# Response phase of a fused attention and ConvNeXt block: high half as a view of the product, low half on VectorE, two-bank gelu and output

## The chip, the core and the metric

The kernel runs on one NeuronCore of a Trainium2 chip. The metric is the device time of the whole program in microseconds (us). Three runs of the kernel before took 2929.64, 2929.57 and 2919.75 us, median 2929.57. One more execution was taken by the profiler; every duration below comes from it.

Names of engines: PE is TensorE (PEld its weight loads), DVE is VectorE, ACT is ScalarE, POOL is GpSimd, SP is SyncE, which only issues DMAs here.

## What is computed

The input has 8 images of 48 channels and 112 x 112 pixels. The first layer is a shifted-window attention block with a 48-192-48 MLP. The second is a ConvNeXt V2 block, and the change touches only its end:

```
y = dwconv7x7(x) + dw_b                       # NCHW, then channels last
y = (y - mean) * rsqrt(var + 1e-6) * ln_g + ln_b
y = gelu(y @ w1.T + b1)                       # 48 -> 192 features
gx = sqrt(sum over the image of y*y)          # one number per feature and image
nx = gx / (mean over features of gx + 1e-6)
y = grn_g * (y * nx) + grn_b + y
out = x + (y @ w2.T + b2)                     # 192 -> 48
```

The second matmul of an image can't begin before the squares of all its pixels are added up, because nx depends on the whole image.

## The kernel before

The program has three phases, one after the other: attention, convolution, response. The response phase (`response_phase`) does what stands above from the normalisation on. An image is cut into 8 strips (STRIPS) and there are N = 64 strips. A strip holds 7 rows of the upper half of the image and 7 of the lower half; the halves are groups g = 0 and 1, at partitions 0 to 48 and 64 to 112, and each has 784 pixels (STRIP), cut into two times 392 (HALF), since a PSUM bank holds 512 float32 values.

Every engine walks over the same steps s = -2 ... N+LAG-1 with an order written out by hand in its `step` function, and the engines meet at counting semaphores. LAG is 10: in step s a strip s gets its first matmul (fc1), and strip s-10 ("old") gets its second (fc2), by when its image is summed. G, the gelu's output, has a ring of 16 strips. So there are three stretches: a fill (steps 0 to 9, fc1 alone), a main part (steps 10 to 63, both) and a drain (steps 64 to 73, fc2 alone). In every eighth step `respond` turns the summed squares of an image into scaled second weights; I call this an image boundary.

In one step:

- SP loads Y (the convolution's output) and RS (its 1/std) for strip s+2, and X2, the block's input, for the old strip.
- DVE multiplies Y by RS into `xh` (float32) and casts it to `xm[0]` (bfloat16, the high half) (`normalise`). POOL subtracts, `xm[1] = xh - xm[0]` (`low`), which is the low half. fc1 is then three bfloat16 matmuls, high by high, low by high, high by low, in float32 accuracy.
- PE does fc1 in three parts t = 0, 1, 2, each with two banks b. Parts 0 and 1 make the first 128 features of the two groups for half t of the pixels (in `ps_f[t]`); their two banks use different row groups of the array, and run side by side. Part 2 makes the last 64 features of both groups (in `ps_m`). The step's order on PE is fc1 part 0, fc2 of the old strip, fc1 part 1, fc1 part 2. fc2 is in float32, reads G, and adds up in the two banks of `ps_o`, of which there is one buffer.
- ACT puts the gelu of each bank into G, six instructions of 392 columns (`features`), and squares and sums group 0's 128 first features (`sum_squares`, 784 columns).
- DVE squares and sums the other two thirds of G (group 1's 128 features, and the last 64 of both groups), one 784-column instruction each, and makes the output from `ps_o`, one instruction for each bank (`finish`).
- POOL issues the two stores of the output.

Of the kernel before, what the change touches and what calls it, by code (L numbers as in the profile page):

```python
# [21 lines left out]
STRIP = WS * IMG  # L22
# [1274 lines left out]
def response_phase(nc, weights, later, x2_dram, y_dram, rs_dram, out_dram, strips):  # L1297

    with ExitStack() as ctx:
        def sb(name, shape, dt=F32):  # L1300
            return ctx.enter_context(nc.sbuf_tensor(name, shape, dt))
# [26 lines left out]
        junk_act = sb("r_junk_act", [128, STRIP])  # L1328
        sums = sb("r_sums", [128, 3, RING])
        total = sb("r_total", [128, 3])  # L1330
        both = sb("r_both", [128, 2])
# [8 lines left out]
        S = sems("cleared y_cleared setup_v setup_t f1 f2 pairs mean_ps xh hi summed summed_act totals "  # L1340
# [25 lines left out]
        def _(sp):  # L1366
# [3 lines left out]
            def step(s):  # L1370
# [10 lines left out]
                if old.real:  # L1381
                    if isinstance(old.n, int) and old.n == 0:
                        wait(sp, S["cleared"], CLEARS)
                    wait(sp, S["out_made"], 2 * (old.n - 1))
# [8 lines left out]
        def _(pool):  # L1393
# [3 lines left out]
            def low(s):  # L1397
                if s.real:
                    wait(pool, S["hi"], s.n + 1)
                    wait(pool, S["f1"], 6 * (s.n - 1))  # L1400
                    nc.gpsimd.tensor_tensor(xm[1][:, s.slot(2), :], xh[:], xm[0][:, s.slot(2), :],  # L1401
                                            ALU.subtract).then_inc(S["lo"], 1)

            def store(s):
                if s.real:
                    wait(pool, S["out_made"], 2 * s.n + 2)
# [13 lines left out]
        def _(dve):  # L1420
# [43 lines left out]
            def sum_squares(s, t):  # L1464

                if s.real:
                    wait(dve, S["ge"], 6 * s.n + (4 if t < 2 else 6))
                    g = G[:, s.raw % RING, t, :]
                    wait(dve, S["summed"], 2 * s.n + t - 1)
                    nc.vector.tensor_tensor_reduce(out=junk[:], in0=g, in1=g, scale=1.0, scalar=0.0, op0=ALU.mult,  # L1470
                                                   op1=ALU.add, accum_out=sums[:, t, s.raw % RING:s.raw % RING + 1]
# [305 lines left out]
```

## Time and profile before

| what | value |
|---|---|
| runs | 2929.64, 2929.57, 2919.75 us, median 2929.57 |
| profiled execution | 2942.04 us, its span 2940.4 us |
| granted PE clock, mean over the span | 0.931 |
| busy over the span | PE 2583.5 (88%), DVE 2032.3 (69%), ACT 1767.5 (60%), POOL 1337.5 (45%) |
| response phase, first fc1 to last output instruction | 2485.4 to about 2926 us after the start |

The page divides the whole program. The response phase is its last 15%, so a busy share of the span says little on it, and the rows below are cut to stretches of the phase. Time runs from the start of the span. A clock of 1.00 is 2.4 GHz, and 0.50 is 1.2 GHz.

### The profile page before, as it was taken

The numbers are of one execution on the slowest core, as the hardware profiler recorded it, in microseconds if no ns is written. First come the engines' busy times: TensorE is split into PE (matmuls) and PEld (weight loads), VectorE is DVE, ScalarE is ACT, GpSimd is POOL, SyncE is SP. The second block draws the span as 40 slices with busy tenths as digits, with TensorE's granted clock in tenths as the row PEclk, the third lists the DMA queues.
The fourth block names the chain that finished last, engine by engine and source line by source line (L and its number), as shares of the span: only waits on it lengthen the run. The fifth ranks groups of instructions, "written<-read, shape, count | busy, mean of one in ns | idle before, by whom it ended". The sixth has DMA issues, their size and how long they took to land. (4 is left out here: it accounts for less than half of the span.)

```text
span 2940.4 us, 81102 instructions
## 1 busy us (share of the span) xinstructions
PE 2583.5 (88%) x30330; PEld 1517.3 (52%) x30330; DVE 2032.3 (69%) x3231; ACT 1767.5 (60%) x3278; POOL 1337.5 (45%) x1333
## 2 busy tenths in 40 slices
PE   3999899898989898998989899899937996889997
PEld 2666565565656565565656556566513553333332
DVE  3767676666666675676667667667568996988984
ACT  1666565565656565565656566566657775655551
POOL 3555454454445454454545445455311333544552
PEclk9989999999899999999999999999958998889988
DMA  3111111111111111111111111111036995777774
GB/s 41 31 27 27 35 32 27 27 33 33 27 27 27 34 33 27 27 39 27 27 27 39 27 27 33 34 27 34 20 70 190 287 288 140 158 179 181 193 173 119
DMA packets 198492, 209.90 MB, mean 71 GB/s; under 512 B 159246, under 2 KB 160131, under 8 KB 198184
## 3 DMA queue, kind: packets, MB, share of 16 engines
q1 hardware_dynamic: 185896, 166.14, 24.1%
q0 software_dynamic: 12288, 39.07, 4.3%
q8 instruction: 264, 4.33, 0.6%
q14 instruction: 44, 0.36, 0.0%
HBM read 124.64 MB, written 80.58 MB: 70 GB/s over the span
## 5 line engine op out<-in xcount | busy, mean ns | idle before, releaser
L348 POOL TENSOR_TENSOR shift<-const_b,qmax 113x588 bf16<-113x588 bf16 x256 | 314.2, 1227 | 253.3 <-DVE qmax L536 253.3
L337 POOL TENSOR_TENSOR xm_l<-xh,xm_h 113x784 bf16<-113x784 f32 x128 | 214.6, 1676 | 463.5 <-DVE xm_h L456 463.5
L647 ACT ACTIVATE P<-ps_t 98x588 f32<-98x588 f32 x256 | 169.6, 662 | 337.9 <-PE ps_t L839 337.3
L375 POOL TENSOR_TENSOR sqb_l<-sq,sqb_h 113x392 bf16<-113x392 f32 x256 | 259.7, 1034 | 142.7 <-DVE sqb_h L439 142.7
L446 DVE TENSOR_TENSOR xh<-xc,rs 113x784 f32<-113x784 f32 x64 | 62.4, 976 | 349.1 <-ACT rs L632 349.0
L678 ACT ACTIVATE G<-ps_m 128x392 f32<-128x392 f32 x384 | 176.4, 501 | 130.9 <-PE ps_m L896 93.8
L830 PE MATMUL ps_t<-u_h,xs_h 113*98 113x147 bf16 x1024 | 222.9, 233 | 0.0
L830 PE MATMUL ps_t<-u_h,xs_l 113*98 113x147 bf16 x1024 | 222.5, 232 | 0.0
L830 PE MATMUL ps_t<-u_l,xs_h 113*98 113x147 bf16 x1024 | 222.4, 232 | 0.0
L536 DVE TENSOR_REDUCE qmax<-ps_s 113x12 f32<-113x588 f32 x256 | 196.3, 767 | 36.4 <-PE ps_s L809 33.4
L639 ACT CAST u_h<-ps_m 113x392 bf16<-113x392 f32 x384 | 177.4, 479 | 67.6 <-PE ps_m L784 66.1
L825 PE MATMUL ps_t<-bias,const_b 113*98 113x294 bf16 x512 | 155.4, 303 | 70.5 <-issue 69.4
L629 ACT ACTIVATE lnv<-ps_m,eps 113x392 f32<-113x392 f32 x256 | 138.6, 584 | 130.2 <-PE ps_m L731 128.6
L385 POOL TENSOR_TENSOR x1b_l<-x,x1b_h 113x392 bf16<-113x392 f32 x128 | 119.0, 930 | 213.0 <-DVE x1b_h L563 213.0
L1556 ACT ACTIVATE r_G<-r_ps_f 128x392 f32<-128x392 f32 x256 | 113.9, 511 | 158.2 <-PE r_ps_f L1607 157.9
L528 DVE TENSOR_TENSOR u_l<-ps_m,u_h 113x392 bf16<-113x392 f32 x384 | 199.2, 556 | 7.6 <-ACT u_h L639 7.6
L1238 PE MATMUL conv_ps<-xp_h,band_now 128*64 128x448 bf16 (+1 forms) x1536 | 189.7, 355 | 16.8 <-DVE band_now L1136 16.8
L1470 DVE CUSTOM_DVE_ANT_0 r_junk<-r_G 128x784 f32<-128x784 f32 x128 | 194.1, 1516 | 5.1
L839 PE MATMUL ps_t<-shift,const_b 113*98 113x294 bf16 x512 | 115.1, 308 | 77.5 <-POOL shift L348 76.6
L1096 POOL DMA_DIRECT2D y_scratch<-y x144 | 75.3, 523 | 219.6 <-ACT y L1183 211.2
L809 PE MATMUL ps_s<-xm_h,u_h 49*49 49x49 bf16 x6144 | 174.8, 186 | 0.0
L1408 POOL DMA_DIRECT2D out_rolled<-r_OUT x128 | 80.5, 633 | 206.7 <-DVE r_OUT L1518 206.4
(252 smaller groups left out, 7941.7 us busy)
## 6 DMA issues: line engine op xcount, KB each, us to landing
xin<-rows_scratch SPq DMA_DIRECT2D x96, 236.0 KB, 5.0
xin<-rows_scratch SPq DMA_DIRECT2D x96, 235.8 KB, 5.3
X<-x_windows SPq DMA_DIRECT2D x128, 147.0 KB, 2.9
x_scratch<-x SPq DMA_DIRECT2D x128, 147.0 KB, 2.8
y_scratch<-y POOLq DMA_DIRECT2D x96, 196.0 KB, 4.2
r_RS<-rs_scratch SPq DMA_DIRECT2D x128, 147.0 KB, 3.5
r_Y<-y_scratch SPq DMA_DIRECT2D x128, 147.0 KB, 3.8
r_X<-x_scratch SPq DMA_DIRECT2D x128, 147.0 KB, 4.0
```

The costliest lines, as they stand in the source:

```text
L337: nc.gpsimd.tensor_tensor(xm[a][1][:, r, :], xh[a][:], xm[a][0][:, r, :], ALU.subtract).then_inc(S["lo"][a], 1)
L348: nc.gpsimd.tensor_tensor(shift[:, j % 2], e, m, ALU.mult).then_inc(S["md"], 1)
L375: nc.gpsimd.tensor_tensor(sqb[a][1][:, cols], sq[a][:, cols], sqb[a][0][:, cols], ALU.subtract).then_inc(S["sq_lo"][a], 1)
L528: nc.vector.tensor_tensor(U[1][:, r, h, cols], ps_m[0:R, b, 0:HALF], U[0][:, r, h, cols], ALU.subtract).then_inc(S["u_lo"], 1)
L536: nc.vector.tensor_reduce(qmax[:, j % 2, :].rearrange("p (b n) -> p b n", b=2), ps_s[0:R, :, 0:2 * HQ].rearrange("p b (n t) -> p b n t", t ...
L639: nc.scalar.copy(U[0][:, s.slot(2), h, HALF * b:HALF * b + HALF], ps_m[0:R, b, 0:HALF]).then_inc(S["u_hi"], 1)
L647: nc.scalar.activation(P[:, j % 2].rearrange("p (b n) h t -> p b (n h t)", b=2), ps_t[0:KEYS, :, 0:2 * HQ], ACT.Exp).then_inc(S["ex"], 1)
L678: nc.scalar.activation(out, ps_m[:, b, 0:HALF], ACT.Gelu).then_inc(S["ge"], 1)
L809: ins = mm(ps_s[lo:lo + TOK, b, at:at + TOK], U[0][lo:lo + C + 1, r, h, TOK * w:TOK * w + TOK], xm[0][0][lo:lo + C + 1, r, TOK * w:TOK * w ...
L830: mm(ps_t[0:KEYS, b, HQ * k:HQ * k + HQ], xs[ws][:, r, w, :], U[ms][:, r, :, TOK * w:TOK * w + TOK], start=False, stop=False)
L1238: ins = mm(ps[s][SIDE * side:SIDE * side + SIDE, k, 0:half * IMG], band_now[0:rows_, s, w, m, :], xp[part][0:rows_, s, side, half * k:half ...
L1470: nc.vector.tensor_tensor_reduce(out=junk[:], in0=g, in1=g, scale=1.0, scalar=0.0, op0=ALU.mult, op1=ALU.add, accum_out=sums[:, t, s.raw % ...
```

## The change

Five things change, all in the response phase. (1) `xh` becomes a double buffer in float32, and the high half is no tile of its own any more: `x_high` is a view of `xh` that takes the upper two bytes of each float32 value, so it is cut off and not rounded. fc1's moving operand then has a step of 4 bytes. (2) The low half is subtracted on DVE, not on POOL. POOL only issues stores in the loop. (3) ACT squares both groups' first 128 features in one instruction of 1568 columns, and DVE only squares the last 64. (4) The gelu takes both banks of a part in one instruction, so ACT waits for both, and fc1 for both to be read. (5) The output of a strip is one DVE instruction over both banks, so it waits for both halves of fc2, and fc2 of the next strip waits for all of it. The sums have two columns, and the small addition after the reduction goes.

```
-        xh = sb("r_xh", [R, STRIP])
-        xm = [sb(f"r_xm_{p}", [R, 2, STRIP], BF16) for p in "hl"]
+        xh = sb("r_xh", [R, 2, STRIP])
+        x_low = sb("r_x_low", [R, 2, STRIP], BF16)
+        x_high = xh[:].bitcast(BF16).rearrange("p r (n t) -> p r n t", t=2)[:, :, :, 1]
+        xm = (x_high, x_low)
...
-            def low(s):
-                if s.real:
-                    wait(pool, S["hi"], s.n + 1)
-                    wait(pool, S["f1"], 6 * (s.n - 1))
-                    nc.gpsimd.tensor_tensor(xm[1][:, s.slot(2), :], xh[:], xm[0][:, s.slot(2), :],
-                                            ALU.subtract).then_inc(S["lo"], 1)
...
                     wait(dve, y_loaded[r], 64 * (s.turn(2) + 1))
-                    wait(dve, S["lo"], s.n)
-                    nc.vector.tensor_tensor(xh[:], Y[:, r, :], RS[:, r, :], ALU.mult).then_inc(S["xh"], 1)
+                    wait(dve, S["f1"], 6 * (s.n - 1))
+                    nc.vector.tensor_tensor(xh[:, r, :], Y[:, r, :], RS[:, r, :], ALU.mult).then_inc(S["xh"], 1)
                     wait(dve, S["xh"], s.n + 1)
-                    wait(dve, S["f1"], 6 * (s.n - 1))
-                    nc.vector.tensor_copy(xm[0][:, r, :], xh[:]).then_inc(S["hi"], 1)
+                    nc.vector.tensor_tensor(x_low[:, r, :], xh[:, r, :], x_high[:, r, :], ALU.subtract).then_inc(S["lo"], 1)
...
-                    for b in range(2):
-                        cols = slice(HALF * b, HALF * b + HALF)
-                        wait(dve, S["f2"], 2 * s.n + b + 1)
-                        nc.vector.scalar_tensor_tensor(
-                            out=OUT[:, s.slot(2), cols], in0=ps_o[0:n, b, 0:HALF], scalar=out_b[:, 0:1],
-                            in1=X2[:, s.slot(2), cols], op0=ALU.add, op1=ALU.add).then_inc(S["out_made"], 1)
+                    wait(dve, S["f2"], 2 * s.n + 2)
+                    nc.vector.scalar_tensor_tensor(
+                        out=halves(OUT[:, s.slot(2), :]), in0=ps_o[0:n, :, 0:HALF], scalar=out_b[:, 0:1],
+                        in1=halves(X2[:, s.slot(2), :]), op0=ALU.add, op1=ALU.add).then_inc(S["out_made"], 1)
...
-                    nc.scalar.activation(junk_act[:], G[:, slot, 0, :], ACT.Square,
+                    nc.scalar.activation(junk_act[:], G[:, slot, 0:2, :], ACT.Square,
...
-                    for b in range(2):
-                        wait(act, S["f1"], 6 * s.n + 2 * t + b + 1)
-                        cols = slice(HALF * (t if t < 2 else b), HALF * (t if t < 2 else b) + HALF)
-                        nc.scalar.activation(G[:, slot, b if t < 2 else 2, cols],
-                                             ps_f[t][:, b, 0:HALF], ACT.Gelu).then_inc(S["ge"], 1)
+                    wait(act, S["f1"], 6 * s.n + 2 * t + 2)
+                    out = G[:, slot, 0:2, HALF * t:HALF * t + HALF] if t < 2 else halves(G[:, slot, 2, :])
+                    nc.scalar.activation(out, ps_f[t][:, :, 0:HALF], ACT.Gelu).then_inc(S["ge"], 1)
...
-                    for b in range(2):
-                        wait(pe, S["out_made"], 2 * (s.n - 1) + b + 1)
+                    wait(pe, S["out_made"], s.n)
+                    for b in range(2):
                         cols = slice(HALF * b, HALF * b + HALF)
```

On DVE the main part's step read as follows before (r_OUT is the output, the rows ISA are the squares and the reading of their sum):

```order
L1518 SCALAR_TENSOR_TENSOR r_OUT<-r_ps_o,r_out_b,r_X 112x392 [waits r_f2,r_stored0,r_x2_loaded0]
L1518 SCALAR_TENSOR_TENSOR r_OUT<-r_ps_o,r_out_b,r_X 112x392 [waits r_f2]
L1459 TENSOR_TENSOR r_xh<-r_Y,r_RS 113x784 [waits r_lo,r_y_loaded0]
L1462 CAST r_xm_h<-r_xh 113x784 [waits r_f1,r_xh]
L1470 ISA r_junk,r_sums<-r_G 128x784 [waits r_summed,r_ge]
L1470 ISA r_sums 128x1
L1470 ISA r_junk,r_sums<-r_G 128x784 [waits r_summed,r_ge]
L1470 ISA r_sums 128x1
```

and the same step of the kernel after on DVE (the L46 rows only set a register or wait):

```order
L1505 SCALAR_TENSOR_TENSOR r_OUT<-r_ps_o,r_out_b,r_X 112x784 [waits r_f2]
L46 ISA
L46 REGISTER_ALU [waits r_y_loaded0]
L1452 TENSOR_TENSOR r_xh<-r_Y,r_RS 113x784 [waits r_f1]
L46 REGISTER_ALU
L1454 TENSOR_TENSOR r_x_low<-r_xh 113x784 [waits r_xh]
L46 ISA
L1462 ISA r_junk,r_sums<-r_G 128x784 [waits r_summed,r_ge]
L1462 ISA r_sums 128x1
```

One output instruction and one square are gone, the cast has become a subtraction, and the wait for fc1 (r_f1) now stands ahead of the product.

On PE the end of the drain read, before (r_w2s are the scaled second weights):

```order
L1640 MATMUL r_ps_o<-r_G,r_w2s_both 112x392 [waits r_out_made]
L1643 MATMUL r_ps_o<-r_G,r_w2s_own 48x392 x2
L1640 MATMUL r_ps_o<-r_G,r_w2s_both 112x392 [waits r_out_made]
L1643 MATMUL r_ps_o<-r_G,r_w2s_own 48x392 x2
L1299 UNCONDITIONAL_BRANCH
```

and after:

```order
L1623 MATMUL r_ps_o<-r_G,r_w2s_both 112x392 [waits r_out_made]
L1626 MATMUL r_ps_o<-r_G,r_w2s_own 48x392 x2
L1623 MATMUL r_ps_o<-r_G,r_w2s_both 112x392
L1626 MATMUL r_ps_o<-r_G,r_w2s_own 48x392 x2
L1299 UNCONDITIONAL_BRANCH
```

The number of matmuls is the same; the wait for the output now stands once for a strip, ahead of its first bank, and the strip before must be read out whole by then.

## Rows read from the trace of the kernel before

**Rows 1.** By stretch: length, busy us (instructions), clock, DMA share, GB/s.

```profile
core 0: us, PE busy (x) PEld busy (x) DVE busy (x) ACT busy (x) POOL busy (x), PEclk, DMA share, GB/s
2485.00:2535.00 50.00, 35.69 (x194) 15.53 (x194) 44.17 (x63) 38.20 (x86) 24.63 (x12) 0.70 0.72 143
...
2530.00:2880.00 350.00, 321.20 (x1638) 109.10 (x1640) 308.73 (x479) 191.11 (x442) 173.83 (x157) 0.92 0.74 180
...
2600.00:2634.00 34.00, 34.00 (x184) 11.25 (x183) 33.03 (x46) 20.03 (x50) 18.84 (x18) 1.00 0.82 202
...
2903.00:2928.00 25.00, 22.28 (x83) 5.92 (x82) 8.76 (x14) 0.00 (x0) 7.96 (x16) 1.00 0.54 163
```

**Rows 2.** Timeline, PE in one step: start, us, instruction, [idle before it].

```profile
2604.74 0.35 PE L1607 MATMUL r_ps_f<-r_xm_h,r_w_own_h 49*128 49x392 bf16 x2
...
2607.06 0.91 PE L1640 MATMUL r_ps_o<-r_G,r_w2s_both 128*112 128x392 f32 x2
...
2610.34 0.35 PE L1607 MATMUL r_ps_f<-r_xm_h,r_w_own_h 49*128 49x392 bf16 x2
```

**Rows 3.** Timeline, DVE and POOL in the same step.

```profile
2605.01 1.15 DVE L1518 SCALAR_TENSOR_TENSOR r_OUT<-r_ps_o,r_out_b,r_X 112x392 f32<-112x392 f32 x2
...
2606.08 0.96 DVE L1459 TENSOR_TENSOR r_xh<-r_Y,r_RS 113x784 f32<-113x784 f32 x1
...
2607.17 0.57 DVE L1462 CAST r_xm_h<-r_xh 113x784 bf16<-113x784 f32 x1
...
2607.65 0.97 DVE L1470 CUSTOM_DVE_ANT_0 r_junk<-r_G 128x784 f32<-128x784 f32 x1
...
2608.36 1.79 POOL L1401 TENSOR_TENSOR r_xm_l<-r_xh,r_xm_h 113x784 bf16<-113x784 f32 x1
...
2608.67 2.32 DVE L1470 CUSTOM_DVE_ANT_0 r_junk<-r_G 128x784 f32<-128x784 f32 x1
...
2610.92 1.15 DVE L1518 SCALAR_TENSOR_TENSOR r_OUT<-r_ps_o,r_out_b,r_X 112x392 f32<-112x392 f32 x2
```

**Rows 4.** Timeline, ACT in the same step.

```profile
2605.44 0.89 ACT L1556 ACTIVATE r_G<-r_ps_f 128x392 f32<-128x392 f32 x2 [2.33 <-PE r_ps_f L1607]
...
2606.97 0.88 ACT L1543 ACTIVATE r_junk_act<-r_G 128x784 f32<-128x784 f32 x1
...
2607.72 0.22 ACT L1543 ACTIVATION_READ_ACCUMULATOR r_junk_act<-r_G 128x1 f32 x1
```

**Rows 5.** Timelines of PE and DVE at the image boundary near 2583 us.

```profile
2582.66 0.38 PE L1622 MATMUL r_ps_o<-r_total,r_eye 128*128 128x1 f32 x2 [1.41 <-DVE r_OUT L1518]
```

```profile
2585.30 0.16 DVE L1494 TENSOR_SCALAR r_mean<-r_ps_o 128x1 f32<-128x1 f32 x1 [0.22 <-PE r_ps_o L1628]
...
2585.69 0.93 DVE L1499 SCALAR_TENSOR_TENSOR r_scale<-r_gx,r_inv,r_grn_g 128x2 f32<-128x2 f32 x1
```

```profile
2587.43 1.64 PE L1640 MATMUL r_ps_o<-r_G,r_w2s_both 128*112 128x392 f32 x2 [2.17 <-DVE r_w2s_both L1507]
...
2590.48 1.65 PE L1640 MATMUL r_ps_o<-r_G,r_w2s_both 128*112 128x392 f32 x2
```

**Rows 6.** Timeline of the drain.

```profile
2896.04 0.16 DVE L1494 TENSOR_SCALAR r_mean<-r_ps_o 128x1 f32<-128x1 f32 x1 [1.63 <-PE r_ps_o L1628]
...
2896.43 0.22 DVE L1499 SCALAR_TENSOR_TENSOR r_scale<-r_gx,r_inv,r_grn_g 128x2 f32<-128x2 f32 x1
...
2897.38 1.65 PE L1640 MATMUL r_ps_o<-r_G,r_w2s_both 128*112 128x392 f32 x2 [1.37 <-DVE r_w2s_both L1507]
...
2903.85 0.91 PE L1640 MATMUL r_ps_o<-r_G,r_w2s_both 128*112 128x392 f32 x2
...
2907.12 0.91 PE L1640 MATMUL r_ps_o<-r_G,r_w2s_both 128*112 128x392 f32 x2
2907.34 0.62 DVE L1518 SCALAR_TENSOR_TENSOR r_OUT<-r_ps_o,r_out_b,r_X 112x392 f32<-112x392 f32 x1 [1.11 <-PE r_ps_o L1643]
```

**Rows 7.** A moving operand with 4-byte steps (the convolution's fill): timeline and stretch.

```profile
2180.89 0.53 PE L1223 MATMUL conv_ps<-split,hot 71*64 71x192 bf16 x4 [1.26 <-DVE band L1128]
```

```profile
2180.00:2190.00 10.00, 2.65 (x20) 0.92 (x20) 10.00 (x7) 10.00 (x7) 0.00 (x0) 0.50 0.09 20
```

More of the change, by code:

```diff
@@ L1323, in response_phase @@
         RS = sb("r_RS", [R, 2, STRIP])
-        xh = sb("r_xh", [R, STRIP])
-        xm = [sb(f"r_xm_{p}", [R, 2, STRIP], BF16) for p in "hl"]
+        xh = sb("r_xh", [R, 2, STRIP])
+        x_low = sb("r_x_low", [R, 2, STRIP], BF16)
+        x_high = xh[:].bitcast(BF16).rearrange("p r (n t) -> p r n t", t=2)[:, :, :, 1]
+        xm = (x_high, x_low)
         G = sb("r_G", [128, RING, 3, STRIP])
         junk = sb("r_junk", [128, STRIP])
[L1328 to L1331, printed above, removed]
+        junk_act = sb("r_junk_act", [128, 2, STRIP])
+        sums = sb("r_sums", [128, 2, RING])
+        total = sb("r_total", [128, 2])
         gx = sb("r_gx", [128, 2])
@@ L1383, in step @@
                         wait(sp, S["cleared"], CLEARS)
-                    wait(sp, S["out_made"], 2 * (old.n - 1))
+                    wait(sp, S["out_made"], old.n - 1)
                     for g in range(2):
@@ L1457, in normalise, with sum_squares @@
                     wait(dve, y_loaded[r], 64 * (s.turn(2) + 1))
[L1458 to L1459 removed]
+                    wait(dve, S["f1"], 6 * (s.n - 1))
+                    nc.vector.tensor_tensor(xh[:, r, :], Y[:, r, :], RS[:, r, :], ALU.mult).then_inc(S["xh"], 1)
                     wait(dve, S["xh"], s.n + 1)
[L1461 to L1464 removed]
+                    nc.vector.tensor_tensor(x_low[:, r, :], xh[:, r, :], x_high[:, r, :], ALU.subtract).then_inc(S["lo"], 1)
+            def sum_squares(s):
                 if s.real:
[L1467 to L1469 removed]
+                    wait(dve, S["ge"], 3 * s.n + 3)
+                    g = G[:, s.raw % RING, 2, :]
+                    wait(dve, S["summed"], s.n)
                     nc.vector.tensor_tensor_reduce(out=junk[:], in0=g, in1=g, scale=1.0, scalar=0.0, op0=ALU.mult,
[L1471 removed]
+                                                   op1=ALU.add, accum_out=sums[:, 1, s.raw % RING:s.raw % RING + 1]
                                                    ).then_inc(S["summed"], 1)
@@ L1480, in add_up @@
                     img, p = image(s), s.raw // STRIPS % 2
-                    wait(dve, S["summed"], 2 * (s.n + STRIPS))
+                    wait(dve, S["summed"], s.n + STRIPS)
                     wait(dve, S["summed_act"], s.n + STRIPS)
                     nc.vector.tensor_reduce(total[:], sums[:, :, STRIPS * p:STRIPS * (p + 1)], AX_X, ALU.add
-                                            ).then_inc(S["totals"], 1)
-                    wait(dve, S["totals"], 2 * img + 1)
-                    nc.vector.tensor_tensor(total[:, 0:1], total[:, 0:1], total[:, 1:2], ALU.add
                                             ).then_inc(S["totals"], 1)
@@ L1528, in step @@
                 normalise(nx2)
-                sum_squares(prv, 1)
             steps(dve, step, N + LAG)
@@ L1597, in fc1 @@
                     if t == 0:
-                        wait(pe, S["hi"], s.n + 1)
                         wait(pe, S["lo"], s.n + 1)
@@ L1601, in fc1 @@
                     ps = ps_f[t]
+                    wait(pe, S["ge"], 3 * (s.n - 1) + t + 1)
                     for b in range(2):
-                        wait(pe, S["ge"], 2 * (3 * (s.n - 1) + t) + b + 1)
                         for k, (w, m) in enumerate(((0, 0), (0, 1), (1, 0))):
@@ L1619, in respond @@
                     if part == 0:
-                        wait(pe, S["totals"], 2 * img + 2)
-                        wait(pe, S["out_made"], 2 * s.n)
+                        wait(pe, S["totals"], img + 1)
+                        wait(pe, S["out_made"], s.n)
                         mm(ps_o[:, 0, HALF:HALF + 1], eye[:], total[:, 0:1], start=True, stop=True)
-                        mm(ps_o[:, 0, HALF + 1:HALF + 2], twins[:], total[:, 2:3], start=True, stop=True
+                        mm(ps_o[:, 0, HALF + 1:HALF + 2], twins[:], total[:, 1:2], start=True, stop=True
                            ).then_inc(S["pairs"], 1)
@@ L1636, in fc2 @@
                     slot = s.raw % RING
+                    wait(pe, S["out_made"], s.n)
                     for b in range(2):
-                        wait(pe, S["out_made"], 2 * (s.n - 1) + b + 1)
                         cols = slice(HALF * b, HALF * b + HALF)
```

13 lines of the change are left out of this document (6 added, 7 removed).

## The prediction

> **What bounds the kernel now.** I read the share by slices first, to see where the response phase lies, then the phase by stretches, then the timelines of one ordinary step, one image boundary and the drain. The whole phase is 441 us of a span of 2940.4 us, so even a tenth of it is 1.5% of the time.
>
> In the main part 350 us hold PE 321 busy at a clock of 0.92 and DVE 309, while ACT has 191 and POOL 174 [rows 1]. Between boundaries, as from 2600 to 2634, PE is busy in every microsecond at full clock. So an ordinary step is bound by PE: the first matmul of fc1 part 1 stands at 2604.74 and again at 2610.34, a period of 5.60 us, of which fc2 is 3.28 (2607.06 to 2610.34) and fc1 2.32 [rows 2]. The reader is to see that DVE's own period is longer: 2605.01 to 2610.92, 5.91 us without a gap [rows 3]. DVE loses 0.31 us a step on PE and pays at the next image boundary, where PE has to wait for it.
>
> Why DVE is so full stands in the same rows. A square of 784 columns takes 0.97 us, and the second one 2.32, though it is the same instruction. POOL's subtraction runs from 2608.36 to 2610.15, and the long square from 2608.67 ends 0.84 after it [rows 3]. It waited 1.35 us for POOL.
>
> At a boundary PE waits 1.41 us for the late output before it can add up the sums (2582.66), and again until the scaled weights are there at 2587.43, 4.77 us later. By then its clock is at half: one bank of fc2 takes 3.05 us (2587.43 to 2590.48) against 1.64, half of 3.28 [rows 2, 5].
>
> **The main part, ordinary steps: 0.** DVE's new step, from rows 3: one square 0.97 and its read 0.11; the product 0.96; the subtraction, which no row has on DVE, taken as the product's 0.96 with 0.12 of waiting between them (the cast came 1.09 after the product's start, 0.13 after its end); the output in one piece, between 1.15 (two pieces as now) and 0.62 plus 0.41 for 392 more columns at the slope of the cheap square, so 1.03. Sum 4.2 us, and no POOL operation to collide with. If the subtraction cost as much as the long square, 2.32, it would be 5.5, still below 5.60; if it went like the cast, 3.8. ACT: two gelus of 392 take 0.89 together, one of 784 about the square's 0.88; spaced as the square and its read are (0.75) that is 2.25 for three, the square of 1568 columns 1.4 to 1.5, the read 0.1, together 3.8 of 5.60 [rows 4]. So both engines lie under PE, whose matmuls are the same in number and size. The waits that are now for both banks fall on buffers that are read long before: ACT idles 2.33 us in each step. What DVE gives back in ordinary steps is worth nothing. Between 0 and -0.1 us a step for PE; I take 0.
>
> The wait for fc1 now stands ahead of the product. Behind it are queued the subtraction and the square; the product is for strip s+2, whose fc1 comes more than one whole step of 5.60 us later, and 3 us are enough. SP's loads wait for the product and so start about 1 us later relative to fc2; they have two steps to land.
>
> **Seven boundaries with fc1 beside them: -19 us, and -7 for the clock.** The DVE lag of 7 x 0.31 = 2.2 us is gone, so the output is ready 1.3 us after fc2's end (worked out under the drain), while fc1's parts 1 and 2, nine of its twelve streams, take 1.7 of the 2.32. The first wait goes: -1.4 (Rows 5 has a typical one). From the adding-up (T) on: DVE does the product and the subtraction first, which wait for fc1 and take 0.96 + 0.12 + 0.96, until T+2.2. Then comes the chain from the mean to the weights. In the drain, with no POOL operation beside it, it takes 1.34 us (2896.04 to 2897.38), its L1499 0.22; at the boundary the same L1499 took 0.93 [rows 5, 6]. So fc2 starts at T+3.5, not T+4.77: -1.3. Together -2.7 a boundary, seven times -19. If DVE were still late by a square (0.97), -1.7 each and -12.
>
> The clock: of PE's idle time of 3.6 us at this boundary, about 1.5 is left. At half clock fc2 of that step costs up to 2 x (3.05 - 1.64) = 2.8 us more; since the clock comes back within it in most cases, I take 2 us for each. If the clock no longer falls that is -14, if it falls as before 0. I take half, -7.
>
> **Fill: -5 us.** In the fill a step had no output, so DVE needed 5.91 - 1.15 = 4.76 us, and PE ran at a mean clock of 0.70 [rows 1, 3]. The new bound is ACT's 3.8 us, or PE at half clock with twice 2.32, less its fixed gaps, 4.2; I take 4.0. That is 0.75 for each of the seven steps in which both squares ran. The first three were shorter already. Bounds: 0 (loads can't follow; their share is 0.72 at 4.76 us a step, 0.86 at 4.0) and -9.
>
> **Drain: +11 us, and +2 for the clock.** Here nothing covers the output. Before, PE filled one bank while DVE read the other, and fc2 of a strip took 3.28 us without a gap (2903.85 to 2907.12) [rows 6]. Now fc2 of the next strip waits for the whole output: DVE started 0.22 us after PE had gone on (2907.34 against 2907.12), then come 1.03 for the output and some 0.05 for the way back, an estimate: 1.3 us. Of ten strips eight have such a transition without fc1 or a boundary in it: +10.4, and the last output ends 0.4 later. With 1.15 for the output it is +12; with the 0.62 of one bank, which is too little, +7.
>
> A rule speaks against the change here. The Trainium skill, TensorE: Matmul & The Clock Gate, section A second HAM failure mode: psum-queue depth-cycling, says that short idle times of PE between groups of matmuls that cycle through PSUM banks make its clock swing between its two levels. By that rule the drain would lose more than its gaps. The trace of before is in favour of it in the fill, where the mean clock is 0.70, and can't show it in the drain, where PE has no gaps and a clock of 1.00 [rows 1].
>
> **Sum.** -19 - 7 - 5 + 11 + 2 = -18 us. The profiled execution took 2942.04, its span 2940.4, so it would become 2924. It stands 12.5 us (0.4%) above the median of the runs. On the median, 2929.57 - 18 = 2912 us.
>
> **The rivals.**
>
> A: as summed, 2912, its own range 2900 to 2921. Chance 0.52.
>
> B: the clock stays up at the boundaries. -19 - 14 - 5 + 11 = -27, 2902. For it: only 1.5 of 3.6 us idle are left. Against it: the rest of that stretch is one-column matmuls and weight loads. Chance 0.13.
>
> C: the clock swings in the drain. fc2 of a strip then takes 6.1 instead of 3.28, for up to ten strips +28, with half of them +14, and no gain at the boundaries: -19 - 5 + 11 + 14 = +1, 2930. For it the fill's 0.70, against it that PE is busy for 3.28 of 4.6 us here. Chance 0.13.
>
> D: the loads become the bound. Their share is 0.82 at 5.6 to 5.9 us a step [rows 1] and would be 0.87 at 5.60. X2 of the old strip is issued last and later than now by 1 us; if the output waits for it by over 1 us, PE waits too. With 5.9 us a step, 54 steps x 0.3 = +16 and the sum is -2, 2928. Chance 0.11.
>
> E, the other side: the view with 4-byte steps streams more slowly. Eight of a step's twelve streams of 392 columns read it (parts 0 and 1 two each, part 2 four), each 392 / 2.4 GHz = 0.163 us. At half rate that is +1.3 us a step and +83 in all, 2995. It turns the sum positive from 18 / 64 = 0.28 us a step, 0.035 us a stream. Against it: the convolution's fill has such an operand, four matmuls of 192 columns, two by two side by side, from start to end in 0.53 us at half clock, which is 0.16 for one stream (192 / 1.2 GHz) and a last one's length [rows 7]. So at 1.2 GHz there is no loss; at 2.4 GHz no row shows a bfloat16 view, but fc2's float32 operand also takes 4 bytes a column. Chance 0.06, and 0.05 for any other loss of some size (the subtraction with its strided operand above 2.5 us would make DVE the bound).
>
> **How the numbers follow.** 0.5% of the median is 14.6 us, about what can be told from no change; faster means under 2914.9. Of A's 0.52 some 0.40 lie under it, all of B: 0.53. A's rest, C and D are the same: 0.36. Slower has E and the rest: 0.11. The range for 8 in 10 reaches from B with its bounds, 2893, to C, D and the runs' own scatter of 10 us, 2933.
>
> **What would show it.** In the profile after: DVE's squares all near 0.97 us; a PE step of 5.60 between boundaries with DVE idle in it; no wait of PE's L1605 (the adding-up) for the output; about 3.5 us from there to fc2; in the drain a gap of 1.3 us before each strip's first L1623 and output instructions of about 1.0 us. It is wrong if a stream of x_high takes over 0.17 us at full clock, if DVE waits for X2, or if the drain's clock is 0.50.

## The result, and the profile after

Seven runs of the kernel after took 2895.08 to 2914.46 us, median 2901.78; seven of the kernel before, beside them, 2918.78 to 2940.01, median 2926.01. The ratio is 0.992 with a 95% interval of 0.9891 to 0.995: faster by 0.8%, 24 us (by the interval 15 to 32). The forecast was 2912 us (18 us less) in a range of 2893 to 2933. Ratios leave out runs that took over 1.5% more than the fastest of the same kernel: one of the fourteen of `e1` below, and one of the seventeen of before beside it.

The profiled executions differ by more, a span of 2895.2 against 2940.4 us. But 21 of those 45 us lie ahead of the response phase, where nothing was changed: its first matmul came at 2464.2, before at 2485.4. So I compare the phase by itself. Let R be the time from the first matmul of fc1 to the end of the last output instruction. R fell from 440.6 to 416.6 us, by 24.0. All readings below are of R and its parts, each from one profiled execution:

| kernel | R | fill, to the first fc2 | from an image's first fc2 to the next one's, seven times | last image's first fc2 to the end |
|---|---|---|---|---|
| before | 440.6 | 49.9 | 52.1 53.5 53.4 53.0 51.9 52.8, 45.4 | 28.6 |
| after | 416.6 | 40.8 | 49.8 48.0 49.1 49.6 48.0 48.0, 45.2 | 38.2 |

The windows of the kernel after, in the columns of [rows 1]: fill, main part, an ordinary stretch, drain.

```profile
2470.00:2499.00 29.00, 20.20 (x147) 7.95 (x145) 23.14 (x32) 29.00 (x41) 0.00 (x0) 1.00 0.95 174
2490.00:2840.00 350.00, 330.44 (x1755) 112.26 (x1751) 228.22 (x336) 241.75 (x311) 55.13 (x111) 0.99 0.85 191
2560.00:2594.00 34.00, 34.00 (x184) 11.01 (x182) 23.35 (x31) 23.18 (x31) 6.03 (x13) 1.00 0.91 207
2850.00:2880.00 30.00, 22.20 (x82) 5.75 (x78) 6.43 (x7) 0.00 (x0) 5.97 (x13) 1.00 0.42 129
```

In the main part DVE went from 309 busy us of 350 to 228 and ACT from 191 to 242; PE is at 0.99 of its clock, before at 0.92 [rows 1]. (This window starts 26 us after the first fc1 and that of before 45 us; from 2509 on, at the same distance, it is DVE 220, ACT 225 and a clock of 0.99.) In the drain PE is busy in only 22.2 of 30 us. An ordinary step on PE, which answers to [rows 2]:

```profile
2560.47 0.91 PE L1623 MATMUL r_ps_o<-r_G,r_w2s_both 128*112 128x392 f32 x2
...
2563.75 0.35 PE L1590 MATMUL r_ps_f<-r_xh,r_w_own_h 49*128 49x392 bf16 x2
...
2566.12 0.58 PE L1623 MATMUL r_ps_o<-r_G,r_w2s_both 128*112 128x392 f32 x1
```

The step is 5.65 us (2560.47 to 2566.12) instead of 5.60. fc2 still takes 3.28 of it, so the 0.05 lies in fc1. DVE in the same step, the answer to [rows 3]:

```profile
2559.95 0.97 DVE L1452 TENSOR_TENSOR r_xh<-r_Y,r_RS 113x784 f32<-113x784 f32 x1 [0.71 <-PE r_ps_m L1594]
2560.96 0.97 DVE L1454 TENSOR_TENSOR r_x_low<-r_xh 113x784 bf16<-113x784 f32 x1
2561.86 0.97 DVE L1462 CUSTOM_DVE_ANT_0 r_junk<-r_G 128x784 f32<-128x784 f32 x1
...
2563.86 1.03 DVE L1505 SCALAR_TENSOR_TENSOR r_OUT<-r_ps_o,r_out_b,r_X 112x784 f32<-112x784 f32 x1 [1.03 <-PE r_ps_o L1626]
```

DVE is now idle for 1.74 us of each step; the output takes 1.03 and starts 0.11 after fc2's end at 2563.75. ACT, the answer to [rows 4], does three gelus and the long square, and idles 1.8:

```profile
2560.67 1.50 ACT L1529 ACTIVATE r_junk_act<-r_G 128x1568 f32<-128x1568 f32 x1
...
2562.17 0.81 ACT L1541 ACTIVATE r_G<-r_ps_f 128x784 f32<-128x784 f32 x1
2564.52 0.82 ACT L1541 ACTIVATE r_G<-r_ps_f 128x784 f32<-128x784 f32 x1 [1.54 <-PE r_ps_f L1590]
2565.60 0.82 ACT L1541 ACTIVATE r_G<-r_ps_m 128x784 f32<-128x784 f32 x1 [0.26 <-PE r_ps_m L1594]
```

An image boundary, the answer to [rows 5]:

```profile
2551.37 0.28 PE L1605 MATMUL r_ps_o<-r_total,r_eye 128*128 128x1 f32 x2
...
2552.57 0.97 DVE L1454 TENSOR_TENSOR r_x_low<-r_xh 113x784 bf16<-113x784 f32 x1
...
2553.48 0.16 DVE L1483 TENSOR_SCALAR r_mean<-r_ps_o 128x1 f32<-128x1 f32 x1
...
2553.87 0.22 DVE L1488 SCALAR_TENSOR_TENSOR r_scale<-r_gx,r_inv,r_grn_g 128x2 f32<-128x2 f32 x1
...
2554.82 0.91 PE L1623 MATMUL r_ps_o<-r_G,r_w2s_both 128*112 128x392 f32 x2 [1.38 <-DVE r_w2s_both L1496]
```

PE no longer waits ahead of the adding-up (L1605, T). L1488 takes 0.22, its form of before took 0.93. The first fc2 stands at T+3.45, before at T+4.77, and its first pair takes 0.91 and not 1.64: the clock is up. Of that chain the subtraction ended at T+2.17 (2.2 was forecast) and the rest, from the mean to fc2, took 1.34 (1.34 was forecast). The drain, the answer to [rows 6]:

```profile
2853.36 0.91 PE L1623 MATMUL r_ps_o<-r_G,r_w2s_both 128*112 128x392 f32 x2 [1.24 <-DVE r_OUT L1505]
2855.00 0.91 PE L1623 MATMUL r_ps_o<-r_G,r_w2s_both 128*112 128x392 f32 x2
2857.94 0.91 PE L1623 MATMUL r_ps_o<-r_G,r_w2s_both 128*112 128x392 f32 x2 [1.24 <-DVE r_OUT L1505]
```

A strip takes 4.58 us (2853.36 to 2857.94) where it took 3.28, and the clock stays at 1.00.

So of the -24.0 us (the parts are rounded), -9.1 lie in the fill with the first boundary, -24.3 in the six periods behind it, -0.2 in the seventh and +9.5 (28.6 to 38.2) in the last stretch.

### The profile page after: what moved, and what is told of

Its sections match the earlier page's. It is cut to its first block and busy times, and to the rows that moved or that the text cites. A ratio compares the mean times of both kernels' runs of the same rounds, so it can differ in the third digit from the quotient of the medians.

```text
span 2895.2 us, 80111 instructions
## 1 busy us (share of the span) xinstructions
PE 2545.9 (88%) x30330; PEld 1501.1 (52%) x30330; DVE 1917.9 (66%) x3031; ACT 1799.3 (62%) x3086; POOL 1192.3 (41%) x1269
## 5 line engine op out<-in xcount | busy, mean ns | idle before, releaser
L1402 POOL DMA_DIRECT2D out_rolled<-r_OUT x128 | 64.0, 503 | 364.7 <-DVE r_OUT L1505 361.9
L852 PE MATMUL ps_v<-wv_h,xs_h 113*98 113x96 bf16 x1024 | 172.2, 219 | 0.8 <-DVE xs_h L517 0.6
L852 PE MATMUL ps_v<-wv_l,xs_h 113*98 113x96 bf16 x1024 | 170.6, 217 | 0.0
L852 PE MATMUL ps_v<-wv_h,xs_l 113*98 113x96 bf16 x1024 | 170.5, 217 | 0.0
```

The source lines that it names most:

```text
L852: ins = mm(ps_v[0:KEYS, 2 * C * k:2 * C * (k + 1)], xs[ws][:, r, QP * j + k, :], wv[ms][:], start=(n == 0), stop=(n == 2))
```

## Experiments: one part undone

Six kernels undo one part of the change, or do one part of it in the kernel before. Six more, in the next section, keep PE busy at the boundaries, four of them with one part undone as well. The periods vary with the clock at each boundary, so I give, beside R, how many of the eight first fc2 pairs ran at half clock (1.5 us or more instead of 0.91). Before it was eight of eight, in the kernel after one of eight, and one between (1.24). That count misses boundaries at which the clock fell only behind the first pair; with the second bank's first pair (1.5 us or more in either) it is before 8, after 3, `e1` 5, `e2` 6, `e3` 8, `e4` 7, `e5` 7, `e8` 8.

Two limits hold for all that follows. Each R comes from one profiled execution. And these kernels ran on three other occasions, on chips 2, 13 and 11, on which the kernel before took 2934.87 (`e1` to `e3`, `e5`), 2939.45 (`e4`, `e6`, `e8`, `e9`) and 2935.75 us (`e10` to `e13`, one run), where it took 2926.01 beside the kernel after. The kernel after was not run again there. Only `e1` and `e9` were run more than once. So what a trace shows of waits and instructions is firm, while a difference in R that is made of the clock may belong to the execution or the chip and not to the edit.

**Output in one instruction for each bank** (`e1`), and the waits on it doubled:

```
-                    wait(dve, S["f2"], 2 * s.n + 2)
-                    nc.vector.scalar_tensor_tensor(
-                        out=halves(OUT[:, s.slot(2), :]), in0=ps_o[0:n, :, 0:HALF], scalar=out_b[:, 0:1],
+                    for b in range(2):
...
+                        wait(dve, S["f2"], 2 * s.n + b + 1)
+                        nc.vector.scalar_tensor_tensor(
+                            out=OUT[:, s.slot(2), cols], in0=ps_o[0:n, b, 0:HALF], scalar=out_b[:, 0:1],
...
```

> The kernel after with the output made bank by bank again, and fc2 waiting for one bank at a time, as before. R is the response phase, from the first fc1 matmul to the end of the last output instruction: 440.6 us before, 416.6 after. Theory: the merged output costs only in the drain, where fc2 of the next strip waits 1.3 us for it, so the drain's period goes from 4.58 back to 3.28 us and R to 406 (-10.5). The main part stays at 5.66 us a step. Rival 1: the gap is made up for elsewhere (stores or loads of X2 can't follow 3.28 us), then R stays over 412. Rival 2: the two short output instructions make DVE late again, then the main part's image period grows over 48.0 us.

Measured: the last stretch is 28.5 us against 38.2, -9.7. Its drain, PE's first matmuls of each bank and DVE:

```profile
2919.47 0.91 PE L1625 MATMUL r_ps_o<-r_G,r_w2s_both 128*112 128x392 f32 x2
2921.10 0.91 PE L1625 MATMUL r_ps_o<-r_G,r_w2s_both 128*112 128x392 f32 x2
2922.74 0.91 PE L1625 MATMUL r_ps_o<-r_G,r_w2s_both 128*112 128x392 f32 x2
```

```profile
2919.58 0.62 DVE L1507 SCALAR_TENSOR_TENSOR r_OUT<-r_ps_o,r_out_b,r_X 112x392 f32<-112x392 f32 x1 [0.92 <-PE r_ps_o L1628]
```

One bank each 1.64 us, without a gap. R is 411.3, not 406: half clock stood at the first three boundaries (periods 50.3, 50.7, 52.0). The periods behind them are 48.0, so two short output instructions do not make DVE late. This profiled execution was the slowest of 14 runs, the one that the ratio leaves out; the drain of `e9`, below, shows the same gain. The median of the 14 is 2913.58 against 2934.87 for before, and the ratio 0.9917 (0.9893 to 0.994) is not told apart from the 0.992 of the kernel after. So the drain's loss is shown in the traces, and not in the runs' time.

**Low half on POOL** (`e2`), DVE keeps the rest:

```
+                    nc.gpsimd.tensor_tensor(x_low[:, r, :], xh[:, r, :], x_high[:, r, :], ALU.subtract).then_inc(S["lo"], 1)
...
-                    nc.vector.tensor_tensor(x_low[:, r, :], xh[:, r, :], x_high[:, r, :], ALU.subtract).then_inc(S["lo"], 1)
```

> The kernel after with the low half subtracted on POOL again, from the view. Theory (the gain is DVE's shorter list, and at a boundary the chain on DVE without a collision): DVE's step is 3.0 us plus 1.35 of waiting for POOL, still below 5.66, so ordinary steps stay; at a boundary the small L1488 collides with POOL again, the scaled weights come 0.7 to 1.0 us later, and the clock falls more often: R 416.6 + 7 x 1 to + 7 x 3 = 424 to 438. Rival (only the length of DVE's list mattered, since it is shorter still here): R 412 to 418.

Measured: R 426.4, +9.8, in the theory's range. Ordinary steps are as in the kernel after. At the boundary the weights' chain meets the subtraction:

```profile
2627.62 1.50 POOL L1403 TENSOR_TENSOR r_x_low<-r_xh 113x784 bf16<-113x784 f32 x1
...
2628.37 0.79 DVE L1495 SCALAR_TENSOR_TENSOR r_scale<-r_gx,r_inv,r_grn_g 128x2 f32<-128x2 f32 x1
```

A two-column DVE instruction took 0.79 instead of 0.22 and ended 0.04 us behind POOL's. T to fc2 is 3.57 to 4.02 against 3.45, so 0.1 to 0.6 later and not the 0.7 to 1.0 that I had expected, and half clock stood at four boundaries of eight. Most of the 9.8 is thus the clock; `e11`, below, has 3 us without it. The Trainium skill, SBUF — State Buffer, section Who interferes with whom, calls the port pair that the two share an exclusive lock; the trace agrees.

**Squares split as before** (`e3`), DVE two thirds, ACT one:

```
-            nc.scalar.activation(junk_act[:], G[:, slot, 0:2, :], ACT.Square,
+            nc.scalar.activation(junk_act[:], G[:, slot, 0, :], ACT.Square,
...
-                sum_squares(s.at(-2))
+                sum_squares(s.at(-2), 2)
...
+                sum_squares(prv, 1)
```

> The kernel after with the squares shared as before: ACT one group's 128 features, DVE the rest in two instructions. Theory: DVE's step becomes 5.2 us without a collision, below 5.66, so ordinary steps stay; the fill is bound by DVE at 4.1 us a step and not by ACT at 3.61: +4; at a boundary the second square stands ahead of the chain: +0.8 x 7 = +6. R 425 to 429, more if the clock falls at boundaries again. Rival (the squares are the gain, since DVE is late again): image period over 52 us and R over 435.

Measured: R 440.1, over the theory's 425 to 429 ("more if the clock falls") and by R on the rival's side. The fill is 44.0 (+3.2) and T to fc2 4.3 (+0.85), as expected, and half clock stood at five of eight. But DVE is not late: PE waits ahead of T at the first boundary (3.5 us, for the sums), and else only at the last, where no fc1 stands beside it. What I had missed is one period of 55.8, the others 50.4 to 51.4. In it DVE stands still once, with its square's data long there:

```profile
2690.72 0.97 DVE L1462 CUSTOM_DVE_ANT_0 r_junk<-r_G 128x784 f32<-128x784 f32 x1
...
2695.98 0.98 DVE L1462 CUSTOM_DVE_ANT_0 r_junk<-r_G 128x784 f32<-128x784 f32 x1 [4.29 <-ACT r_G L1545]
```

The place is the step at which the engines' loop over 16 steps jumps back (step 32). A pause at that step lengthens the third period of most kernels here; in the kernel after it is SP's (6.2 us from the last issue of one step to the first of the next, 2628.91 to 2635.11, where the steps around it have 3.1 to 3.8), and one load of X2 comes late:

```profile
2642.37 1.03 DVE L1505 SCALAR_TENSOR_TENSOR r_OUT<-r_ps_o,r_out_b,r_X 112x784 f32<-112x784 f32 x1 [3.31 <-DMA r_X<-x_scratch]
2643.46 0.91 PE L1623 MATMUL r_ps_o<-r_G,r_w2s_both 128*112 128x392 f32 x2 [1.04 <-DVE r_OUT L1505]
```

It costs the kernel after 1.0 us of PE once (its period of 49.1), and e3 about 4 to 5. That the jump itself makes the pause is my reading of the place; no run took the loop away.

**Gelu for each bank** (`e4`):

```
-                    wait(act, S["f1"], 6 * s.n + 2 * t + 2)
+                    for b in range(2):
+                        wait(act, S["f1"], 6 * s.n + 2 * t + b + 1)
...
-                    wait(pe, S["ge"], 3 * (s.n - 1) + t + 1)
-                    for b in range(2):
+                    for b in range(2):
+                        wait(pe, S["ge"], 2 * (3 * (s.n - 1) + t) + b + 1)
```

> The kernel after with the gelu bank by bank again, six instructions a step. R is the response phase, 416.6 us after. Theory: ACT has room in the main part, so nothing there; in the fill, which ACT bounds at 3.61 us a step, three times 0.77 in place of 0.70 make 3.8: +2. R 417 to 420. Rival (the two-bank gelu delays fc1, which waits for the whole): R under 415.

Measured: R 426.4, a miss. The fill is 42.0 (+1.2, where +2 was expected). The rest is clock: half clock stood at four of the eight first fc2 pairs (periods 50.8 49.4 51.1 48.0 49.6 49.4, 46.8). At the six boundaries between the first and the last T to fc2 is 3.46 to 3.50, as in the kernel after, and PE's matmuls and waits up to there are the same to 0.05 us. Even so two of the six had their first pair at half clock and three more fell behind it, as here, where the kernel after had one of six:

```profile
2637.82 0.91 PE L1625 MATMUL r_ps_o<-r_G,r_w2s_both 128*112 128x392 f32 x2 [1.37 <-DVE r_w2s_both L1496]
...
2639.55 1.65 PE L1625 MATMUL r_ps_o<-r_G,r_w2s_both 128*112 128x392 f32 x2
```

Nothing in the traces ties that to the edit, so the 9.8 us are not shown to be the price of the gelu for each bank.

**High half rounded into a dense tile** (`e5`):

```
+        x_high = sb("r_x_high", [R, 2, STRIP], BF16)
...
+                    nc.vector.tensor_copy(x_high[:, r, :], xh[:, r, :]).then_inc(S["hi"], 1)
+                    wait(dve, S["hi"], s.n + 1)
                     nc.vector.tensor_tensor(x_low[:, r, :], xh[:, r, :], x_high[:, r, :], ALU.subtract)
```

> The kernel after with the high half rounded into a tile of its own by one more DVE instruction, as before, so that fc1's moving operand is contiguous. Theory: the 0.055 us by which a step is longer after (5.655 against 5.600) comes from the 4-byte steps of the moving operand, so a step goes back to 5.60 (-0.055 x 54 = -3) and L1590's and L1594's streams of the high half start 0.163 to 0.167 us apart; the cast adds 0.5 to 0.6 us ahead of the boundary's chain (+4). R 416 to 420. Rival (the 0.055 comes from waits that changed): the step stays at 5.655.

Measured: the step is 5.60 us again:

```profile
2639.68 0.91 PE L1625 MATMUL r_ps_o<-r_G,r_w2s_both 128*112 128x392 f32 x2
...
2642.96 0.35 PE L1592 MATMUL r_ps_f<-r_x_high,r_w_own_h 49*128 49x392 bf16 x2
...
2645.28 0.91 PE L1625 MATMUL r_ps_o<-r_G,r_w2s_both 128*112 128x392 f32 x2
```

So the view's 4-byte steps do cost 0.05 us a step. By the groups of lines (mean ns of one) the matmuls that read the high half take 343, 331, 341 and 334 in the kernel after and 338, 326, 334 and 329 here; spread over the eight streams of a step, 0.055 us is 0.007 us each, too little to see in one row. T to fc2 is 4.04 to 4.11 (+0.6, the copy). R is 425.5, not 416 to 420, with half clock at five of eight.

**The kernel before with the low half on DVE** (`e8`): POOL's `low` is gone, and DVE subtracts behind its cast.

> The kernel before with one change: the low half is subtracted on DVE and not on POOL. Theory (the 1.35 us of waiting are only exchanged for 0.97 of work and 0.12 of waiting): DVE's step stays at 5.8 to 5.95 us and DVE is late at boundaries as before; only the boundary's chain gets shorter, by 0.7 to 1.0 us, and the fill, by 0.3 a step: R 428 to 438. Rival (the collision was the cause): R 425 or less, and PE no longer waits for the output at boundaries.

Measured: R 431.3, in the theory's range, but its reason was wrong: DVE's step is not 5.8 to 5.95. Rows of DVE, which answer to [rows 3]:

```profile
2642.85 0.97 DVE L1464 CUSTOM_DVE_ANT_0 r_junk<-r_G 128x784 f32<-128x784 f32 x1
...
2643.75 1.15 DVE L1512 SCALAR_TENSOR_TENSOR r_OUT<-r_ps_o,r_out_b,r_X 112x392 f32<-112x392 f32 x2
2644.82 0.97 DVE L1451 TENSOR_TENSOR r_xh<-r_Y,r_RS 113x784 f32<-113x784 f32 x1
2645.94 0.57 DVE L1454 CAST r_xm_h<-r_xh 113x784 bf16<-113x784 f32 x1 [0.15 <-PE r_ps_m L1605]
2646.55 0.98 DVE L1456 TENSOR_TENSOR r_xm_l<-r_xh,r_xm_h 113x784 bf16<-113x784 f32 x1
...
2648.45 0.98 DVE L1464 CUSTOM_DVE_ANT_0 r_junk<-r_G 128x784 f32<-128x784 f32 x1
```

Both squares take 0.97; the 2.32 is gone with POOL's operation. DVE's step is 5.60 (2642.85 to 2648.45), with a wait of 0.15 in it: just as long as PE's. The wait ahead of T fell away at five of the six boundaries between the first and the last, as the rival had it (though R is not its 425 or less), yet T to fc2 stayed 4.4 to 4.8, as DVE now has more to do between them. Seven of the eight first fc2 pairs ran at half clock, and at the last boundary the clock fell behind T too (1.11 us, then 1.63). So in this execution POOL's move by itself is worth 9.3 us of R, and it does not bring the clock back.

## Experiments: the clock held up

These kernels put matmuls of 112 columns behind the averaging (L1610, before L1627), whose results nothing reads:

```
+                        for _ in range(24):
+                            mm(ps_o[:, 1, HALF:HALF + 112], w1_both[0][:], w1_both[1][:, 0:112], start=True, stop=True)
```

**The kernel before with 40 of them** (`e6`):

> The kernel before with 40 additional matmuls of 112 columns at each image boundary, in the time in which PE waits for the scaled weights; their output goes to PSUM columns that nothing reads. Theory (part of the gain is the clock): PE's clock stays at 1.00 or comes back earlier, fc2 of the boundary step takes 3.3 us where it took 4.8 to 6.1, and R falls from 440.6 to 425 to 433. Rival (the clock follows something else, or was worth nothing): R 438 to 445, with clock 0.50 in fc2 as before.

Measured: R 428.7, -11.9. One boundary of it, PE and then DVE:

```profile
2584.90 0.38 PE L1622 MATMUL r_ps_o<-r_total,r_eye 128*128 128x1 f32 x2 [1.40 <-DVE r_OUT L1518]
...
2586.51 3.67 PE L1631 MATMUL r_ps_o<-r_w_both_l,r_w_both_h 113*128 113x112 bf16 x40
...
2589.98 0.99 PE L1642 MATMUL r_ps_o<-r_G,r_w2s_both 128*112 128x392 f32 x2
```

```profile
2587.62 1.24 DVE L1499 SCALAR_TENSOR_TENSOR r_scale<-r_gx,r_inv,r_grn_g 128x2 f32<-128x2 f32 x1
```

The wait ahead of T is unchanged, T to fc2 is even 0.3 longer (5.08), and still the six periods fell from 52.8 to 50.9 in the mean: that is what the half clock cost at a boundary in the main part, 1.9 us, or some 2.1 with the longer chain added (0.2 in the mean).

The filling did not keep the clock from falling at this boundary, it brought it back before fc2. Windows, in the columns of [rows 1], over the later part of the 40 matmuls and over fc2:

```profile
2588.00:2590.00 2.00, 2.00 (x25) 2.00 (x22) 1.93 (x5) 1.52 (x4) 0.84 (x1) 0.50 1.01 309
2590.00:2593.30 3.30, 3.30 (x14) 0.94 (x12) 1.05 (x3) 0.00 (x0) 0.00 (x0) 0.97 0.65 133
```

And the clock of before fell earlier than at fc2 at some boundaries. At that of [rows 5] it was down in fc1, right behind T, ahead of the place that is filled here:

```profile
2583.44 0.55 PE L1607 MATMUL r_ps_f<-r_xm_l,r_w_own_h 49*128 49x392 bf16 x2
```

In `e6` the same pair takes 0.34, behind the same wait of 1.4 us. So the clock can fall as early as behind the wait ahead of T, and does not always.

**The kernel after with 24** (`e10`), with the low half on POOL (`e11`), with the squares split as before (`e12`), with the rounded tile (`e13`):

> The kernel after with 24 more matmuls of 112 columns on PE at each image boundary, behind the averaging; they write columns of a bank that nothing reads. R is the time from the first matmul of fc1 to the end of the last output. Theory (the clock): what kept the kernel after above its best is that the clock fell at some boundaries. With PE kept busy every image period from the second on is 48.0 us and R is 413, which is the 403.3 of the kernel with an output per bank and the same filling, and 9.7 for the drain. Rival (per-bank waits): the output per bank also helped in ordinary steps; then periods stay above 48.5 and R is 416 or more though the clock is up.

> The same filling, with the low half subtracted on POOL. Theory (the clock): of the 10 us of R that the move to DVE was worth (426.4 against 416.6), all but 1 to 3 were boundaries at which the clock fell because the scaled weights came 0.1 to 0.6 us later. Held up, R is 414 to 416 and a period 48.0 to 48.6. Rival (the collision itself): POOL's subtraction costs the 10 us through DVE's longer instructions, and R is 421 or more.

> The same filling, with the squares split between the engines as before (DVE two thirds). Theory: 3.2 us more in the fill and 0.85 more at each of seven boundaries, the rest of the 23.5 us seen without the filling was the clock: R 421 to 424, periods 48.8 to 49.2. Rival: DVE with two squares is late in ordinary steps, R 430 or more and periods above 50.

> The same filling, with the high half rounded into a dense tile of its own. Theory: the view's 4-byte steps cost 0.055 us a step, 3 us in 54 steps, and the copy costs 0.6 at each of seven boundaries: R 413 to 415, periods 48.0 to 48.2, a step of 3.96 us between the second matmul of fc2 and the next first one. Rival: the copy costs more by itself, as in the 425.5 without the filling: R 420 or more.

| kernel, PE kept busy | R | fill | periods | last stretch | at half clock (and between, 0.99 to 1.46 us) |
|---|---|---|---|---|---|
| before (`e6`) | 428.7 | 50.5 | 50.7 51.0 51.1 50.9 50.9 50.5, 44.7 | 28.3 | 1 (5) |
| after (`e10`) | 414.7 | 41.6 | 49.5 48.0 48.8 48.0 48.0 48.0, 45.4 | 37.6 | 2 (0) |
| low half on POOL (`e11`) | 417.8 | 41.7 | 49.4 48.5 50.7 48.3 48.1 48.1, 45.7 | 37.4 | 2 (1) |
| squares as before (`e12`) | 427.1 | 44.5 | 50.4 48.8 51.8 48.8 48.9 50.5, 45.2 | 38.2 | 1 (2) |
| rounded tile (`e13`) | 414.4 | 41.7 | 49.4 48.2 49.2 48.2 48.2 48.2, 44.9 | 36.6 | 1 (0) |
| output per bank (`e9`) | 403.3 | 41.5 | 49.9 48.0 48.0 48.0 48.0 48.0, 44.2 | 27.5 | 1 (1) |

`e13` came out as the theory of the clock had it. `e10` did by its periods; by R alone (414.7 for 413) it is as near to its rival's 416. `e11` missed by 2 (417.8 for 414 to 416). Its period of 50.7 has two causes: the clock was down in part at that boundary (a first pair of 1.46 us), which cost 1.6 against the boundary before, and X2 came late behind the loop's jump, which cost 0.8. `e12` missed by 3 (427.1 for 421 to 424), at the jump (51.8, with DVE's 4.3 us pause), and in one period of 50.5 with the clock down in part. By R it lies halfway to its rival's 430, and three of its periods are over 50; what speaks against DVE being late in ordinary steps is that the others are 48.8 and 48.9. With the clock mostly held, then, and one execution each, the rounded tile is worth nothing either way, POOL's place for the subtraction 3 us, and ACT's share of the squares 12 us: 3 in the fill, 5 at six boundaries (0.85 each), 2 more at the pause, and the rest, about 2, clock after all.

**The best of both** (`e9`): the output per bank and the 24 matmuls.

> The kernel after with the output bank by bank, and with 24 additional matmuls of 112 columns at each image boundary, whose output nothing reads. Theory: the clock no longer falls at any boundary, where it fell at two of seven in the profile after; that is worth 2 to 3 us each on top of the bank-by-bank output, and R is 400 to 404. Rival (24 matmuls take longer than the wait of 1.4 us, or one boundary falls because of a late load): R 405 to 412.

Measured: R 403.3, in the theory's range, with every period from the second on at 48.0. Six runs, median 2899.91 us against 2939.45 for before: ratio 0.9862, interval 0.9825 to 0.9899. It beats the kernel before by 1.4%; its interval overlaps that of the kernel after, which it beats by R (13.3 us, or 0.5% of a run). The last stretch alone is 10.1 us shorter than that of `e10`, which has the same filling.

## Why the prediction was right, step by step

The sum said -18 and R fell by 24.0. The runs' medians differ by the same 24, which is closer than they can tell (15 to 32), and in part luck. The time, 2901.78, is that of rival B (2902) and just inside A's 2900 to 2921. It is not B's sum, though: the clock brought about 10 us where B had 14, and fill, boundaries and drain are off by 1.5 to 4 us each.

- **Ordinary steps, 0.** Right for DVE and ACT: the subtraction took 0.97 us on DVE (taken as 0.96), the output 1.03 (1.03), ACT's long square 1.50 (1.4 to 1.5), and the squares are back at 0.97. Mis-sized for PE: +0.055 us a step, 3 us over 54 steps. It is rival E's mechanism at a fifth of the 0.28 us a step from which it would have turned the sum. The convolution's rows [rows 7], which held against E, are at half clock and could not show it.
- **Seven boundaries, -2.7 each.** Right in both halves: the wait ahead of T is gone, and T to fc2 is 3.45 where T+3.5 was forecast. With filling matmuls on both sides the gain is 2.9 us in a period without a pause (50.9 to 48.0), after the view has taken back 0.4 (`e6`'s filling adds 0.3 of its own). The first boundary is an exception: ACT is still behind from the fill there, its table load comes late, and T to fc2 is 5.57 where it was 4.61. The wait of 1.82 us ahead of T is gone, so this boundary gave 0.9 us and not 2.7.
- **The clock, -7.** Mis-sized. I gave back half, since 1.5 us of idle time are left; the clock fell at the first boundary, in part at the fourth, and behind the first pair at the last. The runs with PE kept busy put its worth at about 10 us: they take 11.9 from before and 1.9 from after. With the +2 of the drain, 5 had been summed for the clock, and this is most of what the forecast missed. Rival B's mechanism was nearer than A's half in this execution. But `e4`, with the same waits, had the clock down at five of the six boundaries between, and `e1`, `e2`, `e3` and `e5` lost 8, 9, 13 and 11 us against their filled twins (`e9`, `e11`, `e12`, `e13`), where the kernel after lost 1.9. So how often the clock falls is not settled by the idle time, and the kernel after may have had a good execution; its seven runs speak for the 24 us as a whole, and not for the clock's share. What tips it stays open.
- **The fill, -5.** Mis-sized: -9.1 with the first boundary in it, about -8 without. I had taken 4.0 us a step, between ACT's sum of 3.8 and 4.2 for PE at half clock. The new bound is ACT, at 3.61 us a step, and seven steps at 3.61 for 4.76 are -8:

```profile
2484.95 1.63 ACT L1541 ACTIVATE r_G<-r_ps_f 128x784 f32<-128x784 f32 x2
2486.36 0.94 ACT L1541 ACTIVATE r_G<-r_ps_m 128x784 f32<-128x784 f32 x1
2487.07 1.63 ACT L1529 ACTIVATE r_junk_act<-r_G 128x1568 f32<-128x1568 f32 x1
...
2488.56 1.66 ACT L1541 ACTIVATE r_G<-r_ps_f 128x784 f32<-128x784 f32 x2
```

  From 2484.95 to 2488.56 ACT has no gap, and PE waits for it in each step. The loads followed, just: the DMA share is 0.95, and DVE waits 0.4 to 0.7 us for Y in each of the fill's later steps without being the bound. PE's clock was 1.00 there, before 0.70 [rows 1], though PE is busy in only 20.2 of 29 us:

```profile
2489.65 0.35 PE L1590 MATMUL r_ps_f<-r_xh,r_w_own_h 49*128 49x392 bf16 x2 [1.10 <-ACT r_G L1541]
```
- **The drain, +11 and +2.** Right in the mechanism: the last stretch grew by 9.5 (seven or eight gaps of 1.3), and giving DVE the banks one by one takes 9.7 off again. For the way back from DVE to PE, 0.05 us, the prediction had no row; the period of 4.58 for 3.28 gives 1.30 for the whole gap, as summed. The +2 for the clock did not come, apart from the fall at the last boundary, which the kernel before had as well. Rival C, a clock that swings in the drain, did not occur: every strip has an idle time of 1.24 us, and the granted clock is 1.00. By the rule of the Trainium skill that stood for it (TensorE: Matmul & The Clock Gate, A second HAM failure mode: psum-queue depth-cycling) the clock should have swung here, if it is read as I read it; the measurement decides against that reading, in the drain and in the fill.
- **Rival D**, late loads, came true once, at step 32, for 1 us. The DMA share rose to 0.91 in the ordinary stretch and X2 was in time otherwise. Besides, the product at the first boundary waited 1.3 us for Y (2500.72).

Without the clock the sum was -19 - 5 + 11 = -13, and `e6` to `e10`, the same change with PE kept busy on both sides, is -14.0. That agreement is partly luck, since errors cancel in it: the fill brought -9.0 and not -5, the six periods -15.0 and the seventh +0.7 where -19 stood for seven boundaries, of which the first gave only 0.9, and the view took back 3 us and the late load 1; the last stretch cost 9.3 and not 11.

## What to carry to other kernels

Before work is moved between engines, find which of its instructions runs long only because another engine works beside it: DVE's second square took 2.32 us for 0.97 of work, and moving POOL's operation onto DVE made DVE's step shorter. At a boundary where PE waits, ask what the clock does behind it: here it was about 10 of 24 us, and with cheap filling matmuls fc2 ran at full clock at most boundaries, where a shorter wait alone did that in one execution and not in others. Merging instructions over two banks pays where an engine is short of time (ACT in the fill) and costs where the same buffer is the only one (the drain, 1.3 us a strip), so it may be wanted in one stage and not in the other.

## What the runs showed of the hardware that I had not expected

- A bfloat16 moving operand with steps of 4 bytes costs about 0.007 us in a stream of 392 columns at full clock (a step of 5.65 against 5.60 us, eight such streams in it), and the convolution's at half clock showed none.
- The granted clock was 1.00 through a fill in which PE had a gap of 1.1 us in each 3.6.
- A two-column DVE instruction took 0.22 us with POOL idle, and 0.79, 0.93 and 1.24 (`e2`, before, `e6`) beside POOL's subtraction, each time ending 0.02 to 0.04 us behind it.
- PE's clock fell to 0.50 behind boundaries at which no wait of PE was longer than 1.4 us (`e4`, 1.37), and stayed at 1.00 behind others with the same waits.
- The pause at step 32 costs 1 us in the kernel after and 4.3 us of DVE's time in `e3` and `e12`.
